# Joining the softmax sums of a transformer block's attention across diagonal slots, on one core

## The reference, cut to what matters

```
xn = layernorm(x, g1, be1);  xm = xn * (1 + sc_a) + sh_a
q, k, v = split(xm @ Wqkv)
attn = softmax(where(causal, q @ k.T * 32 ** -0.5, -inf))
x = x + gt_a * ((attn @ v) @ Wproj + bproj)
xn = layernorm(x, g2, be2);  xm = xn * (1 + sc_m) + sh_m
out = x + gt_m * (gelu(xm @ W1 + b1) @ W2 + b2)
```

## Time and profile before

| | us |
|---|---|
| median of 3 runs | 3225.16 (3224.52 to 3227.09) |
| profiled execution, its time | 3225.8 |
| profiled execution, its span | 3223.7 |
| TensorE busy | 3136.2 (97%) |
| VectorE busy | 2330.7 (72%) |
| GpSimd busy | 1735.7 (54%) |
| ScalarE busy | 1189.2 (37%) |

### The profile page before, as it was taken

One profiled execution on the slowest core, in us unless ns is written; L12 is line 12 of the kernel. 1 busy time (PEld: TensorE's weight loads), 2 busy tenths in 40 slices (PEclk: granted clock), 3 DMA queues, 4 the chain that ended last, 5 costly groups with the idle time before them and its releaser, 6 DMA issues.

```text
span 3223.7 us, 68240 instructions
## 1 busy us (share of the span) xinstructions
PE 3136.2 (97%) x24936; PEld 2524.3 (78%) x24936; DVE 2330.7 (72%) x2981; ACT 1189.2 (37%) x2354; POOL 1735.7 (54%) x1385
## 2 busy tenths in 40 slices
PE   8999999999999999999899999999999999999999
PEld 5666666666666676666688889888898888988888
DVE  4678777777877777666777777776777767777673
ACT  3355555555555555566521212122121211212111
POOL 3288877778878778888743333232333323333232
PEclk9999999999999999999999999999999999999999
DMA  6666665666566666666622121221312213122220
GB/s 240 211 178 178 178 189 174 170 184 186 171 190 176 171 174 191 179 178 184 162 64 75 44 78 48 69 72 46 78 47 71 70 47 78 43 74 65 52 65 14
DMA packets 304611, 391.84 MB, mean 122 GB/s; under 512 B 24281, under 2 KB 206073, under 8 KB 304433
## 3 DMA queue, kind: packets, MB, share of 16 engines
q1 hardware_dynamic: 292320, 371.86, 41.1%
q10 hardware_dynamic: 12112, 17.42, 1.6%
HBM read 270.66 MB, written 118.00 MB: 121 GB/s over the span
## 4 chain that ended last, share of the span: by engine, by line
PE 85%; DVE 5%; issue 4%; POOL 3%; ACT 2%; DMA 1%; SPq 0%; POOLq 0%; ACTq 0%; DVEq 0%
PE psH L997 22%; PE psY L1010 22%; PE psA L775 9%; PE psT L829 7%; PE psA L869 7%; PE psP L901 6%; PE psA L779 4%; PE psS L798 3%; DVE mx L1332 2%; PE psA L842 2%; ACT e L1085 1%; DVE psS L1328 1%; PE psA L888 1%; PE psA L747 1%; PE psA L883 1%
## 5 line engine op out<-in xcount | busy, mean ns | idle before, releaser
L1592 POOL TENSOR_TENSOR h_l<-h_full,h_h 128x256 fp32r<-128x256 f32 x512 | 489.7, 957 | 1081.1 <-DVE h_h L1505 1081.1
L1085 ACT ACTIVATE e<-psT 128x512 f32<-128x512 f32 (+1 forms) x1202 | 606.2, 554 | 555.9 <-PE psT L829 537.5
L1332 DVE TENSOR_REDUCE mx<-psS 128x4 f32<-128x2048 f32 (+3 forms) x384 | 666.3, 1756 | 139.5 <-PE psS L798 102.7
L1208 ACT ACTIVATE h_full<-psH,b1c 128x256 f32<-128x256 f32 x512 | 242.9, 475 | 1227.9 <-PE psH L997 1227.9
L997 PE MATMUL psH<-a_h,w1p_h 128*128 128x256 f32 x2048 | 574.9, 281 | 2.2 <-DVE a_l L1500 2.2
L997 PE MATMUL psH<-a_l,w1p_h 128*128 128x256 f32 x2048 | 576.9, 282 | 0.0
L997 PE MATMUL psH<-a_h,w1p_l 128*128 128x256 f32 x2048 | 576.5, 282 | 0.0
L1637 POOL TENSOR_TENSOR es<-e 128x512 f32<-128x512 f32 (+1 forms) x242 | 439.1, 1817 | 160.2 <-ACT e L1085 88.7
L1505 DVE CAST h_h<-h_full 128x256 fp32r<-128x256 f32 x512 | 180.5, 353 | 408.8 <-ACT h_full L1208 406.1
L829 PEld LDWEIGHTS psT<-qst,kst 97*128 97x128 f32 x2404 | 349.4, 189 | 113.6 <-issue 70.2
L829 PE MATMUL psT<-qst,kst 97*128 97x256 f32 (+1 forms) x2404 | 410.8, 290 | 3.8 <-ACT e L1085 3.3
(11 more groups left out here) (118 smaller groups left out, 5175.1 us busy)
## 6 DMA issues: line engine op xcount, KB each, us to landing
qk_split<-qk_hl SPq DMA_DIRECT2D x128, 512.0 KB, 3.5
kst<-qk_split SPq DMA_DIRECT2D x128, 256.0 KB, 4.1
qst<-qk_split SPq DMA_DIRECT2D x128, 256.0 KB, 4.2
xin<-in_x_dram SPq DMA_DIRECT2D x64, 256.0 KB, 3.6
values<-vout ACTq DMA_DIRECT2D x64, 256.0 KB, 2.3
kmx<-qk_split SPq DMA_DIRECT2D x32, 512.0 KB, 4.7
qmx<-qk_split SPq DMA_DIRECT2D x32, 512.0 KB, 6.2
kst<-qk_split SPq DMA_DIRECT2D x128, 128.0 KB, 4.0
```

What stands on the lines that cost most here:

```text
L1085: act.activation(e[:, s % ERING, 2 * hp:2 * hp + 2, 0:w], score_bank(s, hp, with_a)[:, :, 0:w], ACT.Exp, scale=SCALE).then_inc(sem("exp_do ...
L1208: act.activation(h_full[:, m % 4, :], psH[:, m % 4, 0:RA], ACT.Gelu, bias=b1c[:, m:m + 1])\
L1332: reduce = dve.tensor_reduce(mx[:, part, :, qt], psS[:, :, col:col + w], AX_X, ALU.max)
L1592: return pool.tensor_tensor(dst, full, high.bitcast(F32), ALU.subtract)
```

## The change

Three things are changed in the attention stage.

1. In the 13 bodies with `with_a`, the groups of summed slots are (0,1,2), (3), (4,5,6), (7,8), (9) instead of (0,1,2), (3), (4,5), (6), (7), (8), (9). So slots 4 to 6 (the third quarter, with its diagonal) and 7 and 8 (the second) have one sum and one product of 256 columns each, made in `diagonal_sums`. In a diagonal slot that joins a group, GpSimd adds the whole masked first chunk (256 columns a head) to the sum, and the second chunk (128 columns) to its second half. The three other bodies have groups of one slot, as before.
2. GpSimd's order: the first add of a slot that joins a group is issued in the slot's even step (`half_add`), and low parts are formed on odd steps alone, after the add, for items that ended one or two steps before.
3. In `a_high`, VectorE forms the high part as the maximum of the full value and itself, instead of by a copy; both round on writing.

```diff
-SUM_GROUPS = {True: [(0, 1, 2), (3,), (4, 5)] + [(i,) for i in range(6, SLOTS)], False: [(i,) for i in range(SLOTS)]}
+SUM_GROUPS = {True: [(0, 1, 2), (3,), (4, 5, 6), (7, 8), (9,)], False: [(i,) for i in range(SLOTS)]}
...
                 if i in DIAG_SLOTS:
-                    for hd in range(GH):
-                        mm = pe.matmul(psO[HD * hd:HD * (hd + 1), QUART:QUART + P], ones[:],
-                                       e[:, 2 * t % ERING, hd, 0:P], start=False, stop=True, skip_group_check=True)
+                    place, slots, _ = sum_place(h, i, with_a)
+                    first = 0 if len(slots) > 1 else P
+                    if first:
+                        for hd in range(GH):
+                            pe.matmul(psO[HD * hd:HD * (hd + 1), QUART:QUART + P], ones[:],
+                                      e[:, 2 * t % ERING, hd, 0:P], start=False, stop=True, skip_group_check=True)
                     pe.wait_ge(sem("added"), it * SLOTS + i + 1)
                     past(pe, "pe")
                     for hd in range(GH):
-                        mm = pe.matmul(psO[HD * hd:HD * (hd + 1), QUART + P:2 * QUART], ones[:],
-                                       es[:, sum_place(h, i, with_a)[0], hd, 0:P], start=False, stop=True, skip_group_check=True)
+                        mm = pe.matmul(psO[HD * hd:HD * (hd + 1), QUART + first:2 * QUART], ones[:],
+                                       es[:, place, hd, 0:QUART - first], start=False, stop=True, skip_group_check=True)
+                        if hd == 0 and len(slots) > 1:
+                            mm.then_inc(sem("summed"), len(slots) - 1)
...
-                    sums = slot and s // 2 >= 2 and (s // 2 - 2) % SLOTS not in DIAG_SLOTS
+                    sums = slot and s // 2 >= 2 and (s // 2 - 2) % SLOTS in [i for i in SUMS_END[with_a] if i not in DIAG_SLOTS]
...
-                    dve.tensor_copy(qk_hl[:, n % QK_RING, HIGH[n % 2]].bitcast(F32R), qk_hl[:, n % QK_RING, LOW[n % 2]])\
+                    full = qk_hl[:, n % QK_RING, LOW[n % 2]]
+                    dve.tensor_tensor(qk_hl[:, n % QK_RING, HIGH[n % 2]].bitcast(F32R), full, full, ALU.max)\
                        .then_inc(sem("qk_hi"), 1)
...
+            def half_add(u, t, with_a):
+
+                h, i = divmod(t, SLOTS)
+                place, slots, _ = sum_place(h, i, with_a)
+                if i != slots[0]:
+                    if i in DIAG_SLOTS:
+                        pool.wait_ge(sem("masked"), (u * 2 + h) * len(DIAG) + 2 * DIAG_SLOTS.index(i) + 1)
+                    else:
+                        pool.wait_ge(sem("exp_done"), (u * BODY_STEPS + 2 * t + 1) * 2)
+                    pool.wait_ge(sem("added"), u * BODY_SLOTS + t)
+                    pool.tensor_tensor(es[:, place], es[:, place], e[:, 2 * t % ERING], ALU.add)\
+                        .then_inc(sem("half_added"), 1)
...
                 if i != slots[0]:
-                    pool.wait_ge(sem("added"), u * BODY_SLOTS + t)
-                    pool.tensor_tensor(to, to, first, ALU.add).then_inc(sem("half_added"), 1)
                     pool.wait_ge(sem("half_added"), (u * 2 + h) * HALF_ADDS + HALF_ADDED.index(i) + 1)
+                    if i in DIAG_SLOTS:
+                        to = es[:, place, :, P:QUART]
                     pool.tensor_tensor(to, to, second, ALU.add).then_inc(sem("added"), 1)
                     return
...
                     mask(u, s)
-                    if s % 2 == 1:
+                    if s % 2 == 0:
+                        half_add(u, s // 2, with_a)
+                    else:
                         add(u, s // 2, with_a)
-                    item = ended(u, s - 1, with_a, after_a)
-                    if item:
-                        a_low(*item)
+                        for before in (2, 1):
+                            item = ended(u, s - before, with_a, after_a)
+                            if item:
+                                a_low(*item)
```

More of the change, by code:

```diff
@@ L155, in sum_place @@
     return (h * len(groups) + n) % SRING, groups[n], last if n >= SRING else last - SLOTS
-assert all(groups[-2:] == [(8,), (9,)] for groups in SUM_GROUPS.values()) and {8, 9} <= set(DIAG_SLOTS)
+SUMS_END = {with_a: [g[-1] for g in groups] for with_a, groups in SUM_GROUPS.items()}
+assert all({groups[-2][-1], groups[-1][-1]} <= set(DIAG_SLOTS) and groups[-1] == (9,) for groups in SUM_GROUPS.values())
 LAST_SLOT = {CHUNKS[2 * i][0]: i for i in DIAG_SLOTS}
@@ L836, in added_sums @@
                 place, slots, _ = sum_place(h, i, with_a)
-                if i != slots[-1]:
-                    return
                 pe.wait_ge(sem("added"), (u * 2 + h) * SLOTS + i + 1)
```

## The result

The changed kernel takes 3331.03 us (5 runs, 3328.0 to 3335.81) against 3224.52 for the kernel before on the same chip: ratio 1.0326, 95% interval 1.0315 to 1.0338. It is slower by 106 us where 39 had been forecast, and outside the range of 3228 to 3284.

What follows compares the result with a forecast made beforehand. TensorE sets the pace, GpSimd having only 5 us left in the first half. First half +4.0, second -0.9: +3.1 us a body, +1.9 in the last, together +39; 3225.8 + 39 - 0.6 = 3264 us, range 3228 to 3284.

Steps and rivals of the forecast that it cites:

- the sum without idle: First half, GpSimd from slot 0's add to slot 8's, never resting: 42.5 us, ending at 766.1; break-even was 765.8.
- The walk: Step-by-step timeline of one body's engines: first half +4.0 us, second -0.9, giving 3264 us; chance 0.51.
- the old wait of slot 3: In slot 3's step before the change, TensorE stood 1.11 us a body for GpSimd's masks and sum.
- the product of maxima in slot 3's step: TensorE's product, at 740.19 before, waits for VectorE until 741.35, costing about what the old 1.11 us waits cost.
- Products: Four sum products a body removed from TensorE's path at 0.46 us each: -1.84 us a body, -24 us over 13.
- The form: VectorE's high part as max(full, full): 0.69 us alone, +0.28, and it waits for the GpSimd operation in flight.
- rival (b): VectorE's two-operand high part never waits for GpSimd: +1.3 us a body, 3242 us; chance 0.14.
- the step on SyncE: Stores up to 8 us later block loads behind them, but those are wanted some 45 us later: cost nothing.
- the second half: GpSimd needs 5.63 us up to slot 8's product and TensorE leaves 5.84, so no wait: -0.92 us a body.
- part 3: Half adds a step early give back 2.05 us at slot 1; VectorE's casts end 0.28 after GpSimd's operation in flight.
- the clock: TensorE's granted clock, taken as unchanged in the total; a drop within bodies would show the prediction wrong.
- rival (c): Clock falls after TensorE's first wait, losing 3.4 us of work, second wait covered: +4.4 a body, 3282 us; chance 0.16.

Runs made afterwards that it cites:

- early half adds alone: The kernel before, with only the half adds of slots 1, 2 and 5 issued a step early: 3207.7 us, ratio 0.9947.
- filler: Changed kernel plus zero products ahead of the first half's waits at slots 6 and 8: 3341.0 us; 3291.3 us with the key load also a step earlier.
- order and form alone: The changed kernel with the groups of before, keeping the new GpSimd order and the two-operand high part: 3230.2 us, ratio 1.001.
- key load first: The changed kernel with SyncE's load of keys p = 1 issued a step earlier, ahead of the store of item 4: 3312.6 us, ratio 1.0268.

## Why the prediction was wrong

**Right.** The sign, and for the first half its reason: the sum without idle (42.5 us of GpSimd) left no gain there, and joined in that half alone the groups cost most. The walk's first half, +4.0, measured +3.56 in a half at full clock, out of the terms that it had: 2.1 and 2.3 us at slots 6 and 8 against 2.6 and 2.3, with the old wait of slot 3 gone. One term there was too large: the product of maxima in slot 3's step waited 0.45 us (791.00) where the walk had 1.16. Products: 11830 to 10998 matmuls, at 0.46 us for each call removed, close the books. The form: it waits for GpSimd with the same tile twice too. At 786.37 it took 1.65 us, until 788.02, with an add in flight from 785.09 to 787.47, 0.55 after it; rival (b) is out.

```profile
786.37 1.65 DVE L1321 TENSOR_TENSOR qk_hl<-qk_hl 128x512 fp32r<-128x512 f32 x1
```

```profile
785.09 2.38 POOL L1648 TENSOR_TENSOR es<-es,e 128x1024 f32<-128x1024 f32 x1
```

**Failed: the step on SyncE,** "those are wanted a half (some 45 us) later". That held for the other loads, not for the keys p = 1, which go out at step 18 and are read at step 22, four steps on. The prediction listed the store of item 4 as late, and that it blocks the loads behind it, but gave all these loads one time of need. It cost 16.3 us of waits, 18.4 by the experiment.

**Failed: the second half,** "No wait, just: -0.92". GpSimd did have room (busy 42.38 of 50.92 us; forecast 39.7 of 48.8). But I walked slot 8 against TensorE alone and not against VectorE's splits, though part 3 had just shown that each operation of GpSimd holds them. The maxima's waits rose by 28.8 us; the slack there was 0.6 us (816.25 to 816.89 in the kernel before). The join in that half, forecast to save 0.92 us a body, costs 30 us in all over early half adds alone.

**Failed: the clock,** put at nothing in the sum and priced in rival (c) once a body and as partly covered; that it drops within bodies was one of the prediction's own signs of being wrong. It fell behind three places, most often where two stalls lie close together, and cost 53 us of full speed in the profiled run. It was the largest single term. The later experiments show that it can't be priced apart from the waits: the same filler loses 10 us with the late keys and gains 21 without.

By the terms of the sum, in us a body: waits for GpSimd net of the old +2.6 (forecast +3.8), maxima +2.2 (+1.15), keys +1.25 (0), clock +4.1 (0), products -1.84 (-1.84): +8.3 against +3.1; 8.2 measured. The two figures for the maxima are not the same wait: the forecast one is that of slot 3, the measured one is nearly all at the handover of bodies, and joins in the first half alone leave it at 13.1 us. What stays open is why in three of the 13 bodies the split at the boundary just gets past GpSimd (no 1.23 and 2.10 there), and why of equal stalls some lower the clock and others don't.

## What to carry to other kernels

Before work is moved from a busy engine to a half-idle one, count the receiving engine's time in each stage, and walk its queue against every engine that it shares something with, not only the one that is relieved: here the 2.4 us adds also held VectorE. For each instruction that comes later, name what is queued behind its waiter and the first reader of each of these, by the step of that read. And a change may hide a good part: three edits (groups, form, late low parts) cost, and one (early half adds) is worth 0.5% by itself.

## What the runs showed of the hardware

In the changed kernel the granted clock went from 2.4 to 1.2 GHz 24 times in the 13 bodies, for 3.4 or 6.8 us, each time during or just behind a stall of TensorE, mostly the second of two that were some us apart (1.2 then 2.1 us, 1.2 then 1.5). Not every such pair did it: the one of 1.24 and 2.10 us that ends at 1295 us was followed by none. The run with order and form alone had single stalls of up to 1.5 us and the kernel before of up to 1.2, and neither had a fall there. Filling two stalls a body with products of zeros brought the clock from 0.96 (key load first) to 0.99, took away every fall behind them and made the kernel 21 us faster.

And an operation of VectorE that reads one SBUF tile as both inputs stands behind GpSimd's operation in flight just as one with two tiles does: 1.65 us against 0.68 alone, with its end 0.55 us after the add's.
